# Linear attention on one core: scores times values as three fp16 products, and one ScalarE table set for exponential and logarithm

## The reference, cut to what matters

```
q = split(x @ Wq.T); k = split(x @ Wk.T); v = split(x @ Wv.T)
g = log_sigmoid(x @ Wgk1.T @ Wgk2.T + bgk2) / 32
# recurrence over tokens, S is 64 x 128 per head
S_t = diag(exp(g_t)) S_{t-1} + k_t v_t^T ;  o_t = (q_t / 16)^T S_t      # all in fp32
o = o * rsqrt(mean(o*o) + 1e-5) * rms_w
return (o * silu(x @ Wg.T)) @ Wout.T
```

## Time and profile before

| | us |
|---|---|
| median of 3 runs | 1723.2 (1719.59 to 1725.48) |
| the profiled execution, own time | 1716.48 |
| its span in the trace | 1714.4 |
| PE busy | 1638.2 (96% of the span) |
| DVE, ACT, POOL busy | 1146.9, 858.2, 671.4 |
| mean granted clock of PE | 0.989 of full speed |

### The profile page before, as it was taken

One profiled execution on the slowest core, in us unless ns is written; L12 is line 12 of the kernel. 1 busy time (PEld: TensorE's weight loads), 2 busy tenths in 40 slices (PEclk: granted clock), 3 DMA queues, 4 the chain that ended last, 5 costly groups with the idle time before them and its releaser, 6 DMA issues.

```text
span 1714.4 us, 41995 instructions
## 1 busy us (share of the span) xinstructions
PE 1638.2 (96%) x14962; PEld 1106.0 (65%) x14963; DVE 1146.9 (67%) x2505; ACT 858.2 (50%) x1474; POOL 671.4 (39%) x652
## 2 busy tenths in 40 slices
PE   6999999999989999999999999999999989998999
PEld 3665656666567776765565656666566767777666
DVE  6677766666556666656766656666677678776675
ACT  4455434444466555644343334444466566564774
POOL 2342333444122222123342333444244488888243
PEclk9999999999999999999999999999999999998999
DMA  7132323333302111002210123333322033221011
GB/s 249 53 110 84 97 85 98 110 106 104 84 13 38 24 25 24 1 1 84 87 50 26 37 75 96 111 108 101 96 63 48 2 76 77 54 62 40 14 37 50
DMA packets 90149, 115.69 MB, mean 67 GB/s; under 512 B 9296, under 2 KB 76400, under 8 KB 90032
## 3 DMA queue, kind: packets, MB, share of 16 engines
q1 hardware_dynamic: 69680, 71.17, 14.8%
q0 software_dynamic: 20352, 42.88, 8.8%
HBM read 66.11 MB, written 47.90 MB: 67 GB/s over the span
## 4 chain that ended last, share of the span: by engine, by line
PE 81%; DVE 7%; POOL 4%; ACT 4%; issue 3%; DMA 2%; SPq 0%; DVEq 0%; ACTq 0%; POOLq 0%
PE ps L1701 18%; PE ps L1703 18%; PE ps L1702 18%; PE ps L1944 3%; PE ps L1945 3%; PE ps L1717 3%; PE ps L2042 2%; PE ps L1925 2%; PE ps L1926 2%; PE ps L1863 2%; PE ps L1882 2%; PE ps L2199 2%; PE ps L2181 1%; PE ps L2169 1%; PE ps L2047 1%
## 5 line engine op out<-in xcount | busy, mean ns | idle before, releaser
L719 POOL DMA_INDIRECT routed<-work x142 | 136.5, 961 | 234.5 <-DVE work L1456 229.4
L1701 PE MATMUL ps<-later_hi,work 128*128 (+1 forms) x632 | 203.0, 321 | 1.2 <-ACT work L1054 1.0
L1702 PE MATMUL ps<-later_lo,work 128*128 (+1 forms) x632 | 203.0, 321 | 0.0
L1703 PE MATMUL ps<-later_hi,work 128*128 (+1 forms) x632 | 202.9, 321 | 0.0
L1701 PE MATMUL ps<-xt_hi,wsh 128*128 128x512 f16 x512 | 195.1, 381 | 5.3 <-DVE work L1344 3.0
L1702 PE MATMUL ps<-xt_lo,wsh 128*128 128x512 f16 x512 | 195.0, 381 | 0.0
L1703 PE MATMUL ps<-xt_hi,wsh 128*128 128x512 f16 x512 | 194.9, 381 | 0.0
L864 ACT ACTIVATE work<-ps 128x512 f32<-128x512 f32 x128 | 76.4, 597 | 182.4 <-PE ps L1703 182.1
L650 POOL TENSOR_TENSOR rstd<-mv,eps 128x4 f32<-128x4 f32 x49 | 14.7, 300 | 385.9 <-DVE mv L1149 375.1
L1701 PE MATMUL ps<-wsh,work 128*128 128x256 f16 x512 | 140.3, 274 | 4.0 <-ACT work L853 2.7
L1703 PE MATMUL ps<-wsh,work 128*128 128x256 f16 x512 | 140.4, 274 | 0.0
(11 more groups left out here) (247 smaller groups left out, 4234.2 us busy)
## 6 DMA issues: line engine op xcount, KB each, us to landing
work<-expert_x SPq DMA_DIRECT2D x142, 129.0 KB, 2.1
yg<-in_w_later SPq DMA_DIRECT2D x9, 496.0 KB, 3.5
w1q<-in_w_later SPq DMA_DIRECT2D x9, 496.0 KB, 3.7
yg<-in_w SPq DMA_DIRECT2D x8, 512.0 KB, 3.6
values<-wsh SPq DMA_DIRECT2D x8, 512.0 KB, 3.3
later_hi<-values SPq DMA_DIRECT2D x16, 256.0 KB, 4.6
later_lo<-values SPq DMA_DIRECT2D x16, 256.0 KB, 4.7
out_x<-x SPq DMA_DIRECT2D x8, 512.0 KB, 3.0
```

Source lines behind the costliest of these rows:

```text
L719: nc.gpsimd.indirect_dma_start(routed[:, :], bass.IndirectOffsetOnAxis(m.homes[:, i:i + 1], 0), m.t_y[:, i % 4, :], None).then_inc(s[f"til ...
L1701: nc.tensor.matmul(out_, a[0], b[0], start=start, stop=False)
L1702: nc.tensor.matmul(out_, a[0], b[1], start=False, stop=False)
L1703: return nc.tensor.matmul(out_, a[1], b[0], start=False, stop=stop)
```

## The change

The product `A v` is now three fp16 products, `Ahi vhi + Ahi vlo + Alo vhi`. ACT writes the upper halves (a copy to fp16), POOL the lower ones (fp32 minus upper half, to fp16). v and q are scaled by 16 and the epsilon of the norm by 16^4, so that the result stays the same. PE issues the products by kind: for each half of the sequence all of `A v`, then all of `q S`. PE no longer waits for the mask but for POOL's lower halves (`half_lo`). On ACT one table set that has both exponential and logarithm is loaded by hand once per sequence (`exp_and_ln`). Two semaphores of other stages are merged into existing ones.

```diff
+                def lower_values(g):                       # POOL
+                    pool.wait_ge(s["half_hi"], g * 3 + 1)
+                    nc.gpsimd.tensor_tensor(m.v_lo, m.v, m.v_hi, ALU.subtract).then_inc(s["half_lo"], 1)
                 def body(g):                               # POOL
+                    for j in range(2):
+                        pool.wait_ge(s["half_hi"], g * 3 + 2 + j)
+                        nc.gpsimd.tensor_tensor(flat(m.a_lo[j])..., m.whole(g, j),
+                                                flat(m.a_hi[j])..., ALU.subtract).then_inc(s["half_lo"], 1)
                     if not is_last(g):
                         rstd_of(g + N0(n) + 2)
...
                     if g + 3 < NSEQ:
                         second_rows(n - 1, g + 3)
+                    if not is_last(g):
+                        lower_values(g + 1)
...
+                def upper_values(g):                       # ACT
+                    act.wait_ge(s["v_copied"], (g + 1) * TPS)
+                    nc.scalar.activation(m.v_hi, m.v, ACT.Copy).then_inc(s["half_hi"], 1)
+                def upper_scores(g, j):
+                    act.wait_ge(s["masked"], g * 2 + j + 1)
+                    if j:
+                        act.wait_ge(s["half_lo"], g * 3 + 2)
+                    nc.scalar.activation(flat(m.a_hi[j])..., m.whole(g, j), ACT.Copy).then_inc(s["half_hi"], 1)
                 def body(g, u):                            # ACT
+                    upper_scores(g, 0)
                     act.wait_ge(s["kt_ready"], g + 1)
...
-                        low_keys(g + 1)
+                        low_keys(g + 1, lambda: upper_scores(g, 1))
                         softplus(g + 1)
+                    else:
+                        upper_scores(g, 1)
...
                     turned_hi(1)
+                    if not is_last(g):
+                        upper_values(g + 1)
+                        exp_and_ln()
...
-                    for c in range(TPS):                   # PE
-                        if c % 2 == 0:
-                            pe.wait_ge(s["masked"], g * 2 + c // 2 + 1)
+                    for j in range(2):
+                        pe.wait_ge(s["half_lo"], g * 3 + 2 + j)
+                        for c in range(2 * j, 2 * j + 2):
+                            for p in range(GPAIR):
+                                for h in range(2):
+                                    for ah, vh in ((0, 0), (0, 1), (1, 0)):
+                                        nc.tensor.matmul(ps[:, 2 * j + h, block(c, h, p)], a[ah][:, h, c % 2, p], v[vh][:, c, own], ...)
+                        for c in range(max(2 * j, 1), 2 * j + 2):
+                            pe.wait_ge(s["s_step"], g * 5 + 2 * c - 1)
+                            ... (q S of chunk c, as before)
```

More of the change, by code:

```diff
@@ L61 @@
 MASKED = -1e30
+EXP_AND_LN = 6
 ALU = mybir.AluOpType
@@ L397, in l1ffn_space, with flat @@
             return r([2, FU, SEQ], F16), r([2, FU, SEQ], F16), r([RELUS, SEQ])
+        def flat(a):
+            return a.rearrange("p a b c d -> p (a b c d)") if len(a.shape) == 5 else a.rearrange("p a b c -> p (a b c)")
         def gla_space():
@@ L416, in gla_space @@
             m.squares = m.att
+            spare = xn[:, :, 0:D]
+            rooms = [flat(m.att[:, j]) for j in range(2)]
+            m.whole = lambda g, j: (m.lb if is_last(g) else spare) if j else rooms[1].rearrange("p (a d) -> p a d", d=D)
+            halves = [a.bitcast(F16) for a in rooms]
+            m.a_hi, m.a_lo = ([a[:, n * TPS * D:(n + 1) * TPS * D].rearrange("p (h c a t) -> p h c a t", h=2, c=2, a=GPAIR)
+                               for a in halves] for n in range(2))
+            m.v_hi, m.v_lo = (a[:, :].rearrange("p (c d) -> p c d", c=TPS) for a in (w1q, w2q))
             m.o_hi, m.o_lo = at([2, 2, 2, GPAIR, P], F16), at([2, 2, 2, GPAIR, P], F16)
@@ L945, in gla, with low_keys @@
                 s, m = S[n], gla_space()
-                def low_keys(g):
+                def low_keys(g, between=None):
                     act.wait_ge(s["t_ready"], g + 1)
                     nc.scalar.activation(m.t[0:3 * LOW], ps[0:3 * LOW, GLOW, :], ACT.Copy, scale=1 / WS).then_inc(s["t_hi"], 1)
+                    if between is not None:
+                        between()
                     for p in range(GPAIR):
@@ L1071, in step @@
                                 values_rows(g + 1)
-                nc.scalar.activation(m.bv[0], bv_col, ACT.Copy).then_inc(s["bias_hi"], 1)
+                nc.scalar.activation(m.bv[0], bv_col, ACT.Copy).then_inc(halves_set, 1)
                 queries_keys(0, 0, range(2 * KT))
@@ L2034, in body @@
                             ins.then_inc(s["st_ready"], 1)
-                    for c in range(TPS):
-                        if c % 2 == 0:
-                            pe.wait_ge(s["masked"], g * 2 + c // 2 + 1)
-                        if c:
-                            pe.wait_ge(s["s_step"], g * 5 + 2 * c - 1)
[L2040 to L2044, removed]
+                    for j in range(2):
[3 more added lines that the diff above has]
+                                for h in range(2):
+                                    own = slice((2 * p + h) * DV, (2 * p + h + 1) * DV)
+                                    a, v = (m.a_hi[j], m.a_lo[j]), (m.v_hi, m.v_lo)
+                                    for ah, vh in ((0, 0), (0, 1), (1, 0)):
+                                        nc.tensor.matmul(ps[:, 2 * j + h, block(c, h, p)], a[ah][:, h, c % 2, p], v[vh][:, c, own],
+                                                         start=c == 2 * j and p == ah == vh == 0, stop=False, skip_group_check=True)
+                        for c in range(max(2 * j, 1), 2 * j + 2):
+                            pe.wait_ge(s["s_step"], g * 5 + 2 * c - 1)
+                            for p in range(GPAIR):
```

59 lines of the change are left out of this document (34 added, 25 removed).

## The result

The change makes the kernel faster, but by less than half of what the prediction said: 1717.1 us (median, 1710.47 to 1725.02) against 1725.22 (1719.47 to 1731.28), twenty runs of each, a ratio of 0.9958 [0.9946, 0.997]. That is 7 to 8 us instead of 18. The profiled execution after took 1720.05 us with a span of 1718.2, in the upper third of its runs.

A forecast was written before the change was run, and what follows sets the result against it. PE was taken to bound the kernel, busy 39.75 of 40 us per sequence. Gains of 2.65 + 6 x (2.65 - 0.33) + 1.5 + 0 = 18.1 us gave 1698.4 profiled, 1705 against a 1723.2 median; range 1697 to 1718.

The forecast's parts named there:

- The products: PE's outputs per sequence: 48 fp16 products at 0.054 us each, outputs in 4.63 instead of 7.28 us, 2.65 less.
- Rival 1: On PE, fp16 products stream at about 80 ns: 1.25 us less gain per sequence, 1715 us in all; chance 0.14.
- the 64-row kind: PE's scores and `q S` records: 0.058 us each in a long run, since two heads lie in different array rows.
- The changes of kind: PE switching between `A v` and `q S` products: 0.32 us per pair of changes, two pairs left per sequence, 0.64.
- The new wait: ACT's key copies stand behind POOL's first subtraction (1.88 us), so PE's state updates start 0.33 us later per steady sequence.
- Rival 2: POOL's subtraction decides: a 3.3 us subtraction eats the gain, 4.2 us gives 1737; chance 0.10, of which 0.06 slower.
- The last sequence: Outputs wait for POOL's second half and end 11.0 instead of 12.5 us after the scores: 1.5 us less.
- The stage: Gain summed over all sequences of the attention stage, its start and its last sequence included: 18.1 us.
- The start of the stage: Ahead of sequence 0, table loads go while a copy and a load come: 0 us, bounds -0.5 to +1.5.
- the loads alone: ACT's removed table loads are on no path PE waits for: worth 0, only cover for the added copies.
- Rival 3: Statistics chain behind the outputs doesn't move up; PE stops ahead of its transposes up to 2 us per sequence: 1718; chance 0.10.
- 2.65 + 6 x (2.65 - 0.33) + 1.5 + 0: Total gain: sequence 0 in full, six sequences less the new wait, the last sequence, the stage's start: 18.1 us.

The follow-up runs named there:

- r3: The kernel before with only PE's products reordered by kind, still fp32, no halves, no table load: 1705.64 against 1716.51 us, ratio 0.9933.
- r4: The kernel before with only the exponential-and-logarithm table set loaded once per sequence: 1714.55 against 1716.51 us, ratio 0.9986.
- r8: r5 with ACT's first table load behind the low-rank copy and its exponentials ahead of the upper half of v: 1696.64 us, ratio 0.9884 to before.
- r5: The changed kernel plus 64 small fp16 matmuls (128 PE instructions) ahead of sequence 0: 1699.99 us against 1716.06 before, ratio 0.9905.
- r6: The kernel before plus 64 small fp16 matmuls (128 PE instructions) ahead of sequence 0, nothing else: 1727.3 against 1716.06 us, ratio 1.0071.
- r9: The kernel before plus 128 small fp16 matmuls (256 PE instructions) ahead of sequence 0: 1715.91 against 1715.26 us, ratio 0.9991.
- r2: The changed kernel run and profiled once more, nothing altered: 1713.66 us against 1716.51 before, ratio 0.9985.
- r1: The kernel before run and profiled once more, nothing altered: 1718.15 against 1716.51 us.
- r7: The changed kernel with its fp16 products in the old alternating order: 1723.28 us against 1716.06 before, ratio 1.0048.
- r11: r8 with ACT's upper half of the second scores moved behind the two copies of keys: 1692.96 us against 1715.26 before, ratio 0.9867.

## Why the prediction was wrong

- **The products: right.** 0.056 us each (forecast 0.054), outputs in 4.63 (4.63). That the sum fits to 0.01 is luck in part: the products are 0.1 us longer than forecast and the changes of kind as much shorter. Rival 1 is refuted: its 0.08 us stands in no row and in no run, and this stream shows 0.056. That the 64-row kind goes by 0.058 because two heads lie in different rows is a cause that the earlier trace rows doesn't show; single records of the scores before (600.53 to 600.77) fit it: they start in pairs of the two heads, 0.007 us apart, and 0.112 us lie between pairs.
- **The changes of kind: right in kind, somewhat low.** 0.32 us forecast, 0.39 measured in r3. The prediction counted it inside the gain of the halves, 4 x 0.32 of 2.65 us; r3 shows that the order alone gives 13 of the stage's 16.4 us.
- **The new wait: right place, low price.** 0.72 instead of 0.58 us in sequences 1, 3 and 5, since the subtraction takes 2.13 and not 1.88, and 1.0 in 2 and 4, where the mask comes later. The prediction read its steady sequence from one of the early ones. From the scores of sequence 1 to those of the last lie 220.89 us after and 233.31 before: 12.4 gained where 6 x 2.32 = 13.9 was forecast. Rival 2 needed 3.3 us for it and is refuted.
- **The last sequence:** the forecast wait for POOL's second half is there (1.19 us at 759.85). From scores to the next projection it takes 762.39 - 750.71 = 11.68 us, against 12.54 before: 0.9 gained, 1.5 forecast.

```profile
759.85 0.23 PE L2088 MATMUL ps<-w1q,work 128*128 128x128 f16 x1 [1.19 <-POOL work L746]
```

- **The stage:** 16.4 us instead of 18.1.
- **The start of the stage: wrong.** Put at 0 with +1.5 as its bound, it is +1.9: the load by hand holds up the low-rank copy by the full 1.3 us (forecast: 0.6 felt), and the part just ahead grows by 0.6, the upper half of v (18.4 against r4's 15.5) less what the loads that are gone give back (2.3). r8 takes both back. That the loads alone are worth 0 was also not quite so: r4 has 0.8 us in the stage.
- **Rival 3: refuted.** The chain behind the outputs moved up with them: in sequences 0 to 6 PE waits nowhere ahead of the transposes (L2113), and the stage kept its gain.
- **The step that failed** is the sum itself, "2.65 + 6 x (2.65 - 0.33) + 1.5 + 0": it has no term for anything outside the stage. The change adds 128 instructions to PE's program, and the sum counted their time but not their place in the program. That place costs 8.8 us 600 us later (after against r5, and r6 and r9 against before). Without it the kernel gives 16 us (r5: 1716.06 - 1699.99), within the 11 to 25 of the forecast's own range. The measured 1717.1 does lie in the stated 1697 to 1718, but by luck: its upper part was put there for rivals 1 to 3, and none of them happened. The cause could be looked for before the run: the edit shows the longer program, the page before has the 83 packets of queue q8, and waits for `issue` are in the earlier trace rows. Whether the boundaries would meet the weight bursts could have been tried on the trace before; how long PE would stop there shows in no row of it.

What stays open: how the burst delays the fetch (the q8 packet itself took 1.39 us, and such packets take up to 1.4 in quiet stretches too), why PE resumes 1.7 us behind its end (1466.29 + 1.39 to 1469.35), and which other stages gain or lose from the same shift. From 780 to 1225 us, r5 is 2.3 us shorter than r2, but before and r1 differ by 2.7 there as well. The four profiles with the loss (after, r2, r6, r7) have 444.0 to 444.7 us there, the other ten 440.2 to 443.1, so the same shift may cost some microseconds in that part; no run tests it.

## What to carry to other kernels

Count what an edit adds to the *length* of an engine's program as well as to its time. Where an unrolled stage follows, look at waits put down to `issue` in the middle of a run of one line and at what the DMA queues do just ahead of them; some idle instructions ahead of the stage (here 128) test it in one run. Count also at which instruction each wait stands: steps that are multiples of one number tell of a boundary. Try the reordering of an edit without the edit: here grouping products by kind gave 13 of 16.4 us and cost nothing. And where PE waits for a copy that frees a bank, put the copy ahead of a conversion: in r11 that took PE's wait from 0.72 to 0.25 us, and 3.4 us off the stage.

## What the runs showed of the hardware

- PE stood idle at places in its own program: at steps of 256 of its records, five or six such steps apart, it stopped for 1.2 to 2.8 us (r2); five of the six times a packet of 16384 bytes on q8 met a burst of 256 KB transfers just ahead (493 to 589 other packets). Two other packets met such bursts without a stall (572 and 524), and in quiet stretches the same packets cost nothing that shows.
- The effect repeats with the length of the program: against before, +128 instructions harm (212.6, 211.4 us), +192 nearly not (204.5), +256 not at all (203.6, 204.1).
- Changing between fp32 products of 128 rows and of 64 rows costs PE 0.39 us for the change and the change back, though both are fp32 (r3, average of four pairs).
- Small fp16 products with 128 columns and a new weight load each pass at 0.056 us, a quarter of the 512-column row.
